# A layer of linear attention with a gated second branch: the gate's sigmoid moved into the projection, six weight slots for four, one load of O for four

## The reference

```python
xn = layernorm(x)                                  # x: (8, 2048, 2048)
# first branch: attention with decay, NH = 16 heads of 128, blocks of 256 tokens
qkv = silu(xn @ w_qkv.T)                           # per head q, k, v
def step(kv, blk):
    o_inter = (qi * q_decay) @ kv
    o_intra = ((qi @ ki.T) * diag_decay) @ vi
    kv_new  = block_decay * kv + (ki * k_decay).T @ vi
out  = norm_w * out * rsqrt(mean(out * out) + eps) # over all heads
gate = sigmoid(xn @ w_gate.T)
s    = (gate * out) @ w_out.T
# second branch: weights from two sets of 4 bit planes
soft   = sigmoid(pweight) - sigmoid(nweight)
weight = einsum('oin,n->oi', soft, exps * sigmoid(mask)) * scale
g = silu(xn @ weight.T + bias)
return x + s * g
```

## Time and profile before

| | us |
|---|---|
| median of 2 runs | 2466.41 (2464.87 to 2467.95) |
| the profiled execution | 2474.6 |
| its span, core 7, the slowest | 2473.1 |
| spans of the 8 cores | 2434.2 to 2473.1 |
| mean granted TensorE clock by core | 0.887 to 0.898 of full speed |

### The profile page before, as it was taken

The page is one execution under the profiler, slowest core; times in us unless marked ns, Lnnn a source line. Parts: engine busy times, 40 slices in busy tenths (PEclk is TensorE's granted clock), DMA queues, the critical chain, the costliest instruction groups (busy, mean ns, idle before and its releaser), DMA issues.

```text
span 2473.1 us, 22696 instructions; the slowest of 8 cores (2434.2 to 2473.1 us)
## 1 busy us (share of the span) xinstructions
PE 1651.7 (67%) x7928; PEld 768.3 (31%) x7928; DVE 907.9 (37%) x1677; ACT 604.5 (24%) x808; POOL 191.6 (8%) x308
## 2 busy tenths in 40 slices
PE   1112544445359998387787888788888887368896
PEld 1110211212124443143343434333333333123332
DVE  5555455544550000122333332333333333614444
ACT  2225445454541222411222112222222221100000
POOL 0002322222310000000000000000000000110000
PEclk9999766777679999698999999999999999589998
DMA  8218999999981113012222111222222200598554
GB/s 187 102 51 119 157 156 151 163 140 147 158 126 41 39 38 71 0 26 43 43 43 43 36 26 25 43 43 43 43 43 43 43 18 9 109 202 174 166 166 145
DMA packets 176705, 211.75 MB, mean 86 GB/s; under 512 B 74064, under 2 KB 123216, under 8 KB 172496
## 3 DMA queue, kind: packets, MB, share of 16 engines
q0 software_dynamic: 135936, 109.07, 33.6%
q1 hardware_dynamic: 40656, 101.23, 12.6%
HBM read 277.37 MB, written 41.94 MB: 129 GB/s over the span
## 4 chain that ended last, share of the span: by engine, by line
PE 45%; DMA 27%; DVE 11%; issue 7%; ACT 6%; SPq 2%; DVEq 0%; POOL 0%; ACTq 0%; POOLq 0%
PE pfA L586 28%; DMA pnbg<-nwT 11%; DMA pnbg<-pwT 6%; DMA xT_fc<-xT 6%; PE pfA L452 4%; PE pS L452 4%; ACT sq_b L731 2%; DMA outT<-outb 2%; DVE sT_b L682 2%; DVE mneg_c L197 1%; PE pT L618 1%; PE pT L245 1%; SPq L853 1%; PE pS L734 1%; PE pfA L354 1%
## 5 line engine op out<-in xcount | busy, mean ns | idle before, releaser
L586 PE MATMUL pfA<-xnT,wq_sb 128*128 128x512 bf16 x3072 | 735.4, 395 | 50.4 <-ACT q_dim L602 47.3
L586 PEld LDWEIGHTS pfA<-xnT,wq_sb 128*128 128x128 bf16 x3072 | 302.2, 101 | 419.4 <-issue 106.7
L354 PE MATMUL pfA<-xnT,wg_sb 128*128 128x512 bf16 x512 | 144.8, 453 | 317.6 <-DVE gate_stA L364 258.9
L682 DVE TENSOR_TENSOR sT_b<-pS,decT_all 128x512 bf16<-128x512 f32 x128 | 88.4, 691 | 332.4 <-PE pS L670 332.4
L397 ACT ACTIVATE sgp<-pnbg 128x1024 bf16<-128x1024 bf16 x128 | 135.3, 1057 | 198.1 <-DMA pnbg<-pwT 172.9
L354 PEld LDWEIGHTS pfA<-xnT,wg_sb 128*128 128x128 bf16 x512 | 56.7, 113 | 405.3 <-issue 366.8
L739 DVE SCALAR_TENSOR_TENSOR O_st<-pO,csb,gate_h 128x256 bf16<-128x256 f32 x128 | 61.9, 484 | 324.4 <-ACT sq_b L731 321.3
L406 DVE TENSOR_TENSOR sgp<-sgp,sgn 128x1024 bf16<-128x1024 bf16 x128 | 88.6, 693 | 230.7 <-ACT sgn L402 230.6
L913 PE MATMUL pfA<-O_sb,wout_sb 128*128 128x512 bf16 x512 | 129.9, 413 | 39.0 <-DVE s L922 39.0
L402 ACT ACTIVATE sgn<-pnbg 128x1024 bf16<-128x1024 bf16 x128 | 135.3, 1057 | 77.0 <-DMA pnbg<-nwT 71.3
L418 DVE SCALAR_TENSOR_TENSOR Wacc<-sgp,cpos,Wacc 128x1024 f32<-128x1024 bf16 x96 | 123.3, 1284 | 10.3 <-DVE sgp L406 0.5
(11 more groups left out here) (111 smaller groups left out, 1550.6 us busy)
## 6 DMA issues: line engine op xcount, KB each, us to landing
pnbg<-pwT POOLq DMA_DIRECT2D x128, 256.0 KB, 13.3
pnbg<-nwT POOLq DMA_DIRECT2D x128, 256.0 KB, 13.6
wq_sb<-wqkvT POOLq DMA_DIRECT2D x16, 1536.0 KB, 14.4
xtile<-x SPq DMA_DIRECT2D x16, 1024.0 KB, 5.0
xT_fc<-xT SPq DMA_DIRECT2D x16, 1024.0 KB, 7.4
outT<-outb SPq DMA_DIRECT2D x64, 256.0 KB, 3.0
wg_sb<-wgateT POOLq DMA_DIRECT2D x16, 512.0 KB, 15.8
gate_scr<-gate_stA SPq DMA_DIRECT2D x16, 512.0 KB, 8.5
```

Of the source, the lines that this page charges most:

```text
L354: r = e.matmul(pbank[:], wg_sb[b][:, fc * HD:(fc + 1) * HD], xnT[:, fc * T + tg * 512: fc * T + tg * 512 + 512], start=(fc == 0), stop=(fc ...
L586: r = e.matmul(pfA[par][:], wq_sb[hb][:, fc * 384 + sel * 128: fc * 384 + (sel + 1) * 128], xnT[:, fc * T + tg * 512: fc * T + tg * 512 + ...
L682: tst = sch.op("V", (lambda h, jp: lambda e: e.tensor_tensor(out=sT_b[:, jp * 512:(jp + 1) * 512], in0=pS[jp][:], in1=decT_all[:, h * 512: ...
```

## The change

1. A gate head's four banks are evicted by ScalarE with a sigmoid instead of by VectorE with a copy, so that the scratch holds finished gates.
2. The sigmoids of `gate_h` in stage C are removed, and L739 waits for the load of `gate_h` itself.
3. `pnbg` has 12 tiles instead of 8: 6 slots for each of the two weight sets, and the load of unit ui waits for the sigmoid of unit ui - 6.
4. `O_sb` is loaded in one DMA. All matmuls of stage D wait for it.

```diff
-            for i in range(8)]
+            for i in range(2 * NPSL)]                     # NPSL = 6
@@ emit_gate_head
-                tok_gst[h * NTG + tg] = sch.op("V",
-                    (lambda h, gb, tg, pbank: lambda e: e.tensor_copy(
-                        out=gate_st[gb][:, tg * 512:(tg + 1) * 512],
-                        in_=pbank[:]))(h, gb, tg, pbank),
+                tok_gst[h * NTG + tg] = sch.op("S",
+                    (lambda h, gb, tg, pbank: lambda e: e.activation(
+                        out=gate_st[gb][:, tg * 512:(tg + 1) * 512], in_=pbank[:],
+                        func=AF.Sigmoid))(h, gb, tg, pbank),
                     waits=[tok_gmm[(h, tg)], tok_gsd.get(h - 1)], inc=True)
@@ emit_pn_chunk
-                    bg = ui % 4
-                    bq = 4 + ui % 4
+                    bg = ui % NPSL
+                    bq = NPSL + ui % NPSL
-                        waits=[tok_sig.get((ui - 4, 0))],
+                        waits=[tok_sig.get((ui - NPSL, 0))],
-                        waits=[tok_sig.get((ui - 4, 1))],
+                        waits=[tok_sig.get((ui - NPSL, 1))],
@@ stage C, before the loop (the same for head 1) and in it (for head sh + 2)
-        tok_gsig[0] = sch.op("S", lambda e: e.activation(
-            out=gate_h[0][:], in_=gate_h[0][:], func=AF.Sigmoid),
-            waits=[tok_gld[0]], inc=True)
@@ emit_scan_b
-                       tok_gsig[h]], inc=True)
+                       tok_gld[h]], inc=True)
@@ stage D
-        for tg in range(NTG):
-            tok_oload[tg] = sch.op("Q", (lambda tg: lambda e: e.dma_start(
-                out=O_sb[:].rearrange("p (c t) -> p c t", t=T)[
-                    :, :, tg * 512:(tg + 1) * 512],
-                in_=o_dram[:, :, tg * 512:(tg + 1) * 512].rearrange(
-                    "c p t -> p c t")))(tg),
-                waits=(tok_c_done + [tjoin, tsjoin]) if tg == 0 else [],
-                inc=True, sem=f"olo{tg}")
+        tok_oload = sch.op("Q", lambda e: e.dma_start(
+            out=O_sb[:].rearrange("p (c t) -> p c t", t=T),
+            in_=o_dram.rearrange("c p t -> p c t")),
+            waits=tok_c_done + [tjoin, tsjoin], inc=True, sem="olo")
-                    waits=[tok_wout[fc], tok_oload[tg],
-                           tok_ev3.get((gidx - 4, "s"))], inc=True)
+                    waits=[tok_wout[fc], tok_oload, tok_ev3.get((gidx - 4, "s"))], inc=True)
```

More of the change, by code:

```diff
@@ L165, in build_program @@
     esPN = contextlib.ExitStack()
+    NPSL = 6
     pnbg = [esPN.enter_context(nc.sbuf_tensor(f"pnbg{i}", [128, D // 2], BF16))
-            for i in range(8)]
+            for i in range(2 * NPSL)]
     sgp = [esPN.enter_context(nc.sbuf_tensor(f"sgp{i}", [128, D // 2], BF16))
@@ L557, in build_program @@
         tok_wq[0] = tok_wq0
-        tok_gsig = {}
         tok_gld[0] = sch.op("Q", lambda e: e.dma_start(
@@ L570, in build_program @@
                 inc=True, sem="gld1")
-            tok_gsig[1] = sch.op("S", lambda e: e.activation(
-                out=gate_h[1][:], in_=gate_h[1][:], func=AF.Sigmoid),
-                waits=[tok_gld[1]], inc=True)
         tkv0 = {}
@@ L799, in build_program @@
                         inc=True, sem=f"gld{sh % 2}")
[L800 to L804, removed]
             if ph is not None:
@@ L850, in build_program @@
                 inc=True, sem=f"wou{fc}")
-        tok_oload = {}
-        for tg in range(NTG):
-            tok_oload[tg] = sch.op("Q", (lambda tg: lambda e: e.dma_start(
-                out=O_sb[:].rearrange("p (c t) -> p c t", t=T)[
-                    :, :, tg * 512:(tg + 1) * 512],
-                in_=o_dram[:, :, tg * 512:(tg + 1) * 512].rearrange(
-                    "c p t -> p c t")))(tg),
-                waits=(tok_c_done + [tjoin, tsjoin]) if tg == 0 else [],
-                inc=True, sem=f"olo{tg}")
+        tok_oload = sch.op("Q", lambda e: e.dma_start(
+            out=O_sb[:].rearrange("p (c t) -> p c t", t=T),
+            in_=o_dram.rearrange("c p t -> p c t")),
+            waits=tok_c_done + [tjoin, tsjoin], inc=True, sem="olo")
         tsr2 = sch.op("S", lambda e: e.activation(
```

## The result

| | before | after |
|---|---|---|
| median | 2468.19 | 2428.32 |
| ratio, with its 95% interval | | 0.9826 (0.9798 to 0.9855) |
| the profiled execution | 2474.6 | 2422.86 |
| spans of the 8 cores | 2434.2 to 2473.1 | 2397.0 to 2421.0 |

The medians are those of 10 and 11 executions. In some executions of either kernel the cores of one die run some per cent longer at a lower granted clock; the medians include them, the ratios and intervals leave them out. The ratio is 43 us of 2468 (36 to 50); 50 were forecast. The table cuts the profiled executions of all kernels of this study at the same instructions: the first gate matmul, the first matmul of the second branch, the first projection matmul, the issue of O's load, and the end. Each number is the median over the 8 cores.

What follows compares the result with a forecast made beforehand. The prediction took waits that differ by stage, not a busy engine, as the bound. Its terms, -3.6 - 7 - 5 - 5 - 16.2 - 13 = -50 us, gave 2416 against the median of 2466.4, range 2396 to 2442.

Steps and rivals of the forecast that it cites:

- End of the weight stage, -3.6: Weight stage's end: with ScalarE evicting the gate, TensorE starts head 15 at 729.2 instead of 732.76, -3.6 us.
- The blocked rival: Weight stage: gate evictions wait for TensorE and hold up ScalarE's sigmoids, so DMA starves; +52 us, 2518, chance 0.04.
- Start, -7: Kernel start: six slots let four more transfers land during the layer norm, 4 x 1.8 us, -7 us.
- Steady part, -5: Middle of the weight stage: the deeper queue raises the DMA share slightly; -5 us, between 0 and 20.
- Before the first head, -5.0: Scan's start: two sigmoids and one table load vanish from ScalarE, so the silu's load moves earlier, -5.0 us.
- Head ends, -16.2: Scan, 14 head ends: TensorE's column sums wait less for the square on ScalarE, -16.2 us of 91.3.
- O's load, -13: Last stage: O in one load with 4 KB packets lands earlier, so the next chunk's loads go out earlier; -13 us.
- From there the stage is a serial chain: Last stage after chunk 1's loads are issued: load and VectorE work in series, 14 periods of 17.5 us on average.
- lengthen the next two periods by about 4: Last stage: more weights are left over after O's load and take about 4 us back from the 17 gained.
- 2435: Rival: O's load and the deeper queue's steady part give nothing, -32 us in all; chance of nothing from O 0.26.
- 2421: Weight stage: the longer queue only moves GpSimd's wait, steady part 0; counted within the forecast, no chance of its own.
- the first rival: Large packets and the deeper queue give more: O at 2165, steady part 12 to 15 us; -66 us, 2401, chance 0.18.

Runs made afterwards that it cites:

- gate: Kernel before with the gate's sigmoid at the eviction on ScalarE and none in the scan; four slots, four loads of O. Ratio to before 0.9823.
- slots: Kernel before with six slots instead of four for each weight set, nothing else. Ratio to before 0.9981.
- the three kernels with the sigmoids: The kernel before, `slots` and `oload`, which all keep the gate_h sigmoids in the scan; scan 1148.9 to 1152.5 us.
- The kernels with the large sigmoid: Kernel after with a 128x2048 sigmoid added at 14 head ends, without or with the wait for gate_h; scan 1128.6 and 1142.6 us.
- oload: Kernel before with one load of O instead of four, nothing else. Ratio to before 0.9942.
- sig_full_wait: Kernel after with a 128x2048 sigmoid at 14 head ends that waits for the load of gate_h; scan 1142.6 us against 1126.8 in after.
- undo_o: Kernel after with O's load put back into four. Ratio to before 0.9767, last stage 335.3 us against 328.8 in after.
- sig_wait: Kernel after with a one-element sigmoid at 14 head ends that waits for the load of gate_h; scan 1128.0 us against 1126.8 in after.
- sig_full_nowait: Kernel after with a 128x2048 sigmoid at 14 head ends that waits for nothing; scan 1128.6 us against 1126.8 in after.

## Why the prediction was right, and where a term was not

The time, 2428.32, lies in the range of 2396 to 2442, and the direction was right. 43 us came instead of 50, of which the stages show 46. By terms:

- **End of the weight stage, -3.6.** As the step said: from ScalarE's last sigmoid to TensorE's next matmul 5.3 us became 1.7. The eviction took 0.60 us a bank (0.585 and 0.602 by bank), as the nearest row had it. The blocked rival did not occur: no eviction of heads 1 to 14 waited for TensorE, and the stage became no longer. The four of head 0 did wait, which the step did not name: on core 2 ScalarE was idle for 8.1 us and three times 2.9 there, with 12 transfers in flight.
- **Start, -7.** Measured -6 (236.6 to 230.9), and 230.8 to 232.3 in all kernels with six slots; and with 3 slots +11 for six transfers fewer. The price per transfer was 1.4 to 1.8 us, where 1.8 was forecast.
- **Steady part, -5.** Not confirmed. Six slots alone show nothing, three slots lose some 5 us. The stage's medians after (496.1) and before (505.6) differ by 9.5 us; 3.6 of it is the end, and the rest is within what identical code gave (to ScalarE's last sigmoid 482.8 before, 483.6 in `gate` and 487.7 in `slots`). The step chose well in staying near 0, but 0 to -2 would have been the number. The extra wait that it expected came: on core 7 GpSimd waits 52.1 us for TensorE ahead of the gate weights, 33.0 before, and the stage became no longer.
- **Before the first head, -5.0.** TensorE's wait, 47.3 on core 7 in the earlier trace rows, is 44.4 there; the median of the cores fell from 46.7 to 42.9 us, by 3.8. The silu's table load is now the only one.
- **Head ends, -16.2.** The wait for the square fell from 91.3 to 74.3 on core 7, 17.0 us, and the reading by regular waits held within one. Core 7 was the longest, though: in the median of the cores it fell from 88.9 to 74.2, 14.7 us. Yet the scan fell by more than the 21 us of both steps: by 26, or 21 to 26 if the three kernels with the sigmoids are taken (1148.9 to 1152.5). The rest is matmul time. On core 2 the projections went from 731.8 us busy to 722.3, from 394 ns a matmul to 390, for the same number of the same matmuls. The kernels with the large sigmoid show that it hangs on the stall. On core 5, first without the wait and then with it:

```profile
L582 PE MATMUL pfA<-xnT,wq_sb 128*128 128x512 bf16 x3072 | 722.4, 390 | 47.3 <-ACT q_dim L598 44.3 <-DMA g_scr<-g_st 3.0
```
```profile
L582 PE MATMUL pfA<-xnT,wq_sb 128*128 128x512 bf16 x3072 | 732.2, 394 | 45.6 <-ACT q_dim L598 41.7 <-DMA g_scr<-g_st 3.9
```

  The code of TensorE is the same in both; only its stall at the head ends differs (3.7 us at the longest against 1.0). Core 5 had the longest one: over the six cores whose trace has all 3072 matmuls the medians are 722.7 and 727.3 us, 5 apart, and 732.5 and 722.2 for before and after, 10 apart. Where the 10 us lie is seen at a head end. The kernel before, core 7, and a window of it in the form of the earlier trace rows:

```profile
1348.00 4.57 PE L586 MATMUL pfA<-xnT,wq_sb 128*128 128x512 bf16 x16
...
1356.68 0.35 PE L734 MATMUL pS<-sq_b,ones_bf 128*1 128x256 bf16 x1 [2.47 <-ACT sq_b L731]
1356.97 5.18 PE L586 MATMUL pfA<-xnT,wq_sb 128*128 128x512 bf16 x16
```
```profile
1357.00:1361.00 4.00, 4.00 (x13) 1.53 (x13) 1.22 (x5) 0.00 (x0) 0.00 (x0) 0.61 0.00 0
```

  The same head end in the kernel after, core 2:

```profile
1317.39 4.88 PE L580 MATMUL pfA<-xnT,wq_sb 128*128 128x512 bf16 x16
...
1324.44 0.27 PE L728 MATMUL pS<-sq_b,ones_bf 128*1 128x256 bf16 x1 [0.51 <-ACT sq_b L725]
1324.64 3.63 PE L580 MATMUL pfA<-xnT,wq_sb 128*128 128x512 bf16 x16
```

  Sixteen projection matmuls take 3.6 us at the full clock. The first group after the transposes is slower in both kernels (granted clock 0.57 from 1346 to 1350 us before, 0.63 from 1317 to 1321 after). In the kernel before, the group behind the stall is slow again: the granted clock was back at 1.00 from 1350 to 1353 us and is 0.61 from 1357 to 1361. Counted matmul by matmul, such a second stretch of projection matmuls over 500 ns instead of 379 (more than 6.5 us behind the last transpose) occurs at 1 to 7 head ends of every core in before, `slots`, `oload` and `sig_full_wait`, and at none on any core in after, `gate`, `undo_o`, `sig_wait` and `sig_full_nowait`. The stalls in front of these stretches were 1.7 to 5.5 us; in the kernels without a second stretch the longest is 1.5. On core 7 it is 53 matmuls at some 0.25 us extra, 13 us, and the projections there fell by 13.3 us (735.4 to 722.1). So the extra time is matmuls at the lower of the two clock levels (1.2 GHz), to which the clock fell a second time after the stall. The step priced the stall and forgot that a stall can cost matmul time too.
- **O's load, -13.** This is the term that was mis-sized: 5 in the profile after, 6.6 by the medians of the seven kernels with large packets and after's order of loads (328.8) against the four with small ones (335.4). The step took its numbers from core 7, where the loads of chunk 1 went out as late as on any core (75.4 us after O's issue, 75.3 on core 2, 66.5 in the median). From O's issue to the issue of the load of g:

| us | chunk 1 | chunk 2 | chunk 3 | chunk 4 | chunk 15 |
|---|---|---|---|---|---|
| before, core 7 | 75.4 | 101.5 | 121.4 | 137.9 | 320.2 |
| after, core 7 | 55.2 | 86.9 | 114.3 | 132.8 | 310.2 |
| before, median of the cores | 66.5 | 95.8 | 119.6 | 137.4 | 316.1 |
| after, median of the cores | 58.3 | 87.0 | 113.3 | 130.7 | 310.9 |

  On core 7 the kernel after reads:

```profile
2073.04 0.38 SPq L840 DMA_DIRECT2D O_sb<-o_scr  x1
...
2128.25 1.29 SPq L880 DMA_DIRECT2D g_fc<-g_scr  x1
```

  So on core 7 the loads of chunk 1 came 20 us earlier, even more than the 17 of the step, but only 5 of them were left at chunk 4. In the median of the cores it was 8 us at chunk 1 and 7 at chunk 4. The 75.4 us of core 7 were the end of a spread (59.1 to 75.4 over the cores before) that is mostly made up three chunks later (133.5 to 142.0) without any change. What failed is "From there the stage is a serial chain", by which a microsecond at chunk 1 is one at the end, together with a start read from one late core. The other part, "lengthen the next two periods by about 4", is 13 on core 7 (26.1 and 19.9 us became 31.6 and 27.4) but 2 in the medians. Why a late core catches up was not followed.

  The step also had the wait wrong. It took TensorE to be held by O, landing after 35 us. O landed after 29.0 to 35.6 us, but the first matmul came at 34 to 43 us after O's issue instead of 30 to 32, later than before on all eight cores and held by `wout_sb`. By the equal counts in the earlier trace rows it could be worked out: the 2048 packets of the first weights come one for one with O's 2048, and land when O does, or after. Nor was a 4 KB packet as cheap as the 172 ns of the step: 87.4% of 16 x 15 us over 1051 packets is 200 ns.

By the Trainium skill (DMA: Bandwidth & Descriptors, Queues, rings and completion order) an engine takes turns between queues by packets; 1051 and 1054 packets agree with it. The prediction weighed this rule only for what it gives to O. It takes the same from the other queue, on which TensorE's first matmul depends just as much.

The rivals 2435 (nothing from O, nothing from the queue's depth) and 2421 (the steady part alone gives nothing) both came nearer in the time than the forecast, each within 8 us, and neither in its mechanism: O's load did give 5 to 7. That the total came as near as it did is in part luck. O's load was forecast 6 to 8 us too large and the steady part up to 5, and the 10 us of matmul time that no step had made up for most of it. One sum is off: half of 0.52 and the 0.18 of the first rival give 0.44 for faster, not 0.46.

## What to carry to other kernels

Where a queue of large and one of small packets share the DMA engines, price what the small one loses, piece by piece in the order in which it is needed; a load that lands early is worth little if its partner lands late. Work on an engine that waits for a load is almost free up to the moment at which somebody needs the engine, so wait and work have to be added up before either is judged. Take a period from the median of the cores and not from one: a core that is late in the first chunk can be back with the others by the fourth, and a gain measured there is not a gain at the end. And look at the order within the issuing queue first: loads that stood behind the stores of the chunk in work cost 39 us here, more than all of O's load could bring.

## What was not expected of the hardware

- Packets were served one for one from two queues also when their sizes were 4 KB and 256 bytes: 1051 against 1054, 87.4% and 18.2% of 16 engines' time.
- SP was held while it issued. The load of g behind four loads of O took 13.03 us to issue before (core 7), and behind one load of 8.4 MB still 12.81 us on core 2 and 10.68 on core 7, while O's own took 0.38.
- A casting stream of the same length answers little to its depth: 6, 8 or 12 transfers in flight gave weight stages of 506, 502 and 501 us, with the gate on ScalarE.
- A stall of TensorE at the head ends costs more than itself: some 10 us of matmul time in 3072 matmuls beside 15 us of stall, given back by the change (731.8 to 722.3 on core 2) and taken again by the large sigmoid with the wait (722.4 to 732.2 on core 5). At 1 to 7 head ends of a core the granted clock fell to the lower level a second time, behind stalls of 1.7 to 5.5 us; in the kernels whose stalls stay within 1.5 us it never did.
